# Attention and routed experts on one core: where the value product stands among the scores

## The chip, the cores and the metric

The kernel runs on one core of one Trainium2 chip. The metric is the device time of one execution in microseconds (us); of several runs the median is taken. Engines are TensorE (PE in the profile, its weight loads PEld), VectorE (DVE), ScalarE (ACT), GpSimd (POOL) and SyncE (SP).

## What is computed

A transformer layer on x of 8 x 512 x 128: attention with 16 heads of width 8, a residual and a layer norm, then 8 routed experts of which each token takes two, one shared expert, a residual and a layer norm. The change lies in the attention; the projection is reshaped in such a way that a head of the reference is a block of 32 rows of x with 16 columns of heads in it.

```python
qkv = (x @ w_qkv + b_qkv).reshape(B, N_HEADS, S, 3 * HEAD_DIM)
q, k, v = jnp.split(qkv, 3, axis=-1)
scores = jnp.einsum('bhqd,bhkd->bhqk', q, k) * scale
attn = jax.nn.softmax(scores, axis=-1)
vals = jnp.einsum('bhqk,bhkd->bhqd', attn, v)
vals = vals.transpose(0, 2, 1, 3).reshape(B, S, N_HEADS * HEAD_DIM)
x = layernorm(x + vals @ w_out + b_out)
x = layernorm(x + ffn(x))
```

## The kernel before

Four heads are a *quad*; there are 32, four to a batch of 512 tokens. All engines run the same list of stages (`run_stages`, L318), one per quad, with a few ahead of the first and one behind the last. Stage q does three things at once: the scores A of quad q+2 (`scoreA`, L1012), of which VectorE takes the maxima over the keys (L946); the scores B of quad q (`scoreB`, L1026), which are the same scores with keys and queries exchanged and the maximum subtracted by two more rows of the operands, and which ScalarE exponentiates into `prob` (L919); and the value product of quad q-1 (`pvp`, L1051), in fp32, four heads side by side in the columns of TensorE's array, summed over four chunks of keys in one PSUM bank.

A stage has 8 steps (`at` 0 to 7); head j = at // 2, half u = at % 2. TensorE's program (`attention_tensor`, L986) is an order written out by hand: in each step score A, score B, score A, score B, then the step's *jobs*, and in the odd steps (u = 1) behind them four matmuls of the value product. The two scores B of a step go to the two banks of `scoreB`, c = 0 and c = 1. A score B waits until the exponential of the score that used its bank before is done (L1025):

```python
need(pe, exp_done, 16 * q + 2 * at + c - 1)
```

A score A waits for the maxima of the step before the last (L1011). The value product of step 1 waits for the exponentials of the stage before, for the values (`v_ready`) and for the copy of the last product out of PSUM (`pv_copied`, L1047 to L1049).

The jobs share one PSUM bank, `shared`; a job starts only when the one before was read (`job_read`, L509). `Jobs.at` (L74) says which job stands in which step:

- step 0: the output projection `proj` (L542), in the third quad of a batch;
- step 1: `mT`, the transposition of the maxima (L530), read by VectorE, which writes them negated (L605, L607); SyncE then stores them into the operand rows (L760) and goes on to the loads of the stacks `qs` and `ks` for quad q+3 (L776, L780);
- step 2: `counts` of the router (L503, L504), in the second quad of a batch;
- step 3: `valsT`, the transposition of a finished value product (L534), which VectorE divides by the sums (L593, L599);
- step 4: `xT`, the transposition of a tile of x (L512);
- step 5: `x1T` (L547), in the fourth quad of a batch; ScalarE copies it (L578);
- step 6: `qkv`, the projections for a later quad (L518, L519, L523), which ScalarE reads with three instructions (L568, L572);
- step 7: `oT` (L537), in the second quad, read by a ScalarE copy (L576); `gate` (L553), in the fourth, read by a ScalarE exponential (L582).

ScalarE's program (`attention_scalar`, L899) starts each stage with the copy of the value product of the stage before out of `pvp` (L911), which waits for its last matmul (`pv_done`), and goes on with the 16 exponentials, with the jobs that it reads behind those of their step. VectorE's (`attention_vector`, L932) takes one pair of maxima per step and then that step's jobs and the router's or the norm's small operations. An engine runs its instructions in the order of its program. The experts follow when the attention is done, on the same core; the change does not touch them.

Of the kernel before, what the change touches and what calls it, by code (L numbers as in the profile page):

```python
# [110 lines left out]
def layer(nc, x, w_qkv, b_qkv, w_out, b_out, wg, ws1, ws3, ws2, we1, we3, we2, out):  # L111
# [26 lines left out]
    with ctx:  # L138
        def sb(name, shape, dt=F32):
            return ctx.enter_context(nc.sbuf_tensor(name, shape, dt))  # L140

        def psum(name, shape):
            return ctx.enter_context(nc.psum_tensor(name, shape, F32))

        def sem(name):
            return ctx.enter_context(nc.semaphore(name))
# [42 lines left out]
        v = sb("v", [P, 2, 4, NCH, 32])  # L189
        prob = sb("prob", [P, 2, 4, NCH, 512])  # L190
# [52 lines left out]
        pvp = psum("pvp", [P, 512])  # L243
# [23 lines left out]
        v_ready = sem("v_ready")  # L267
        b_ready = sem("b_ready")
        exp_done = sem("exp_done")
        pv_done = sem("pv_done")  # L270
        pv_copied = sem("pv_copied")
# [24 lines left out]
        def need(eng, s, value):  # L296

            if isinstance(value, int) and value <= 0:
                return
            eng.wait_ge(s, value)  # L300
            if not isinstance(value, int) and eng.engine in ALONE:


                eng.sem_inc(passed, 1)

        def has(b, i, ahead):

            return not isinstance(b, int) or 0 <= 4 * b + i + ahead < QUADS
# [9 lines left out]
        def run_stages(eng, stage):  # L318

            for s in range(-4, 8):  # L320
                stage(s // 4, s % 4)
            with eng.Fori(2, B - 1) as b:
                for i in range(4):
                    stage(b, i)
            for s in range(QUADS - 4, QUADS + 1):
                stage(s // 4, s % 4)
# [355 lines left out]
        def turn_x(pe, b):  # L682

            pe.wait_ge(x1_loaded[b], 16)

            need(pe, xT_low_done, b)
            for c in range(NCH):
                ins = pe.transpose(xT_bank[:, c * P:(c + 1) * P], xsum[:, b, c, :], ident[:])
            ins.then_inc(xT_ready, 1)
# [296 lines left out]
        def attention_tensor(pe):  # L986

            pe.wait_ge(setup, 2)
            for n in range(4):
                pe.matmul(pvp[:, 0:P], ident[:], ident[:], start=True, stop=True)  # L990

            def warm(times, columns):

                for n in range(times):
                    pe.matmul(pvp[:, 0:columns], wq[:], w_raw[:].rearrange("p c k d -> p (c k d)")[:, 0:columns],  # L995
                              start=True, stop=True)

            def stage(b, i):
                q = 4 * b + i
                if isinstance(b, int) and q == -2:  # L1000
                    warm(8, 3 * P)
                if has(b, i, 2):

                    pe.wait_ge(stack_loaded[i % 2], 16 * STACK_DMAS * (2 * b + i // 2 + 2))
                def score_a(at, c):

                    if has(b, i, 2):
                        st, j, qc = (i + 2) % 4, at // 2, at % 2 * 2 + c

                        if c == 0:  # L1010
                            need(pe, max_done, 8 * (q + 2) + at - 1)  # L1011
                        ins = pe.matmul(scoreA[:, at % 2, c], qs[0:KR, st, j, qc * P:(qc + 1) * P],  # L1012
                                        ks[0:KR, st, j, :], start=True, stop=True)
                        if c == 1:
                            ins.then_inc(a_ready, 1)

                def score_b(at, c):

                    if has(b, i, 0):
                        j, kc = at // 2, at % 2 * 2 + c  # L1020
                        if at == 0 and c == 0:

                            pe.wait_ge(m_loaded, 32 * (q + 1))

                        need(pe, exp_done, 16 * q + 2 * at + c - 1)  # L1025
                        pe.matmul(scoreB[:, c], ks[0:KM, i, j, kc * P:(kc + 1) * P], qs[0:KM, i, j, :],  # L1026
                                  start=True, stop=True).then_inc(b_ready, 1)

                for at in range(8):
                    j, u = at // 2, at % 2  # L1030
                    score_a(at, 0)
                    score_b(at, 0)
                    score_a(at, 1)
                    score_b(at, 1)
                    for kind, bb, ii in jobs.at(b, i, at):
                        if kind == "xT" and isinstance(b, int) and q == -3 and at == 7:
                            warm(1, 3 * P)
                        pe_job(pe, kind, bb, ii)
                    if isinstance(b, int) and q in (-2, -1) and not jobs.at(b, i, at) or \
                            isinstance(b, int) and q == 0 and u:  # L1040
                        warm(1, 2 * P)

                    if isinstance(b, int) and q == QUADS and at == 4:
                        turn_x(pe, 0)
                    if u == 1 and has(b, i, -1):
                        if j == 0:
                            pe.wait_ge(exp_done, 16 * q)  # L1047
                            pe.wait_ge(v_ready, q)
                            need(pe, pv_copied, q - 1)  # L1049
                        for h in range(4):  # L1050
                            ins = pe.matmul(pvp[32 * h:32 * h + 32, :], v[:, (i - 1) % 2, h, j, :],  # L1051
                                            prob[:, (i - 1) % 2, h, j, :], start=(j == 0), stop=(j == 3))
                        if j == 3:
                            ins.then_inc(pv_done, 1)

            run_stages(pe, stage)


# [601 lines left out]
```

## Time and profile before

| | |
|---|---|
| median of 3 runs | 690.12 us (687.95 to 690.82) |
| the profiled execution | 686.2 us, of which its span is 684.5 |
| busy: PE, DVE, ACT, POOL | 640.4, 548.9, 424.2, 269.4 us (94, 80, 62 and 39% of the span) |
| scores A, scores B, value products on PE | 512 x 386 ns, 512 x 387 ns, 1024 x 611 ns |
| exponentials on ACT | 512 x 600 ns, 278.7 us |
| maxima on DVE | 256 x 1219 ns, 304.5 us |
| mean granted clock of TensorE | 0.980 |

Matmuls are pipelined, and the profile models their ends; so the distance from one start to the next says more than a duration, and a busy TensorE may be one that waits. The starts are read from timelines, whose columns are: start in us, length of the group in us, engine, line, operation, what it writes and reads, shapes, and the number of instructions; in brackets stands how long the engine was idle before it and what ended that.

### The profile page before, as it was taken

Reading aid. Unit: us, or ns where it says so; the run is one execution under the profiler, and the core shown is the slowest. Engines: PE = TensorE matmul, PEld = TensorE weight load, DVE = VectorE, ACT = ScalarE, POOL = GpSimd, SP = SyncE. Lnnn points to the kernel's source line nnn. Section 1 sums busy time; section 2 is a strip of 40 time slices with the busy share of each in tenths; the row PEclk is TensorE's granted clock in tenths of the full one; section 3 lists DMA queues with packets and bytes.
Section 4 is the critical chain, followed back from the end, with each engine's and each line's share of the span. In section 5 each row is a group of like instructions: output and inputs, shape, how many; then the busy total and the mean of one; then the engine's idle time right before and its main releaser. Section 6 shows DMA issues by size and latency. Waiting matters only on the chain.

```text
span 684.5 us, 16202 instructions
## 1 busy us (share of the span) xinstructions
PE 640.4 (94%) x4653; PEld 320.8 (47%) x4653; DVE 548.9 (80%) x1272; ACT 424.2 (62%) x973; POOL 269.4 (39%) x402
## 2 busy tenths in 40 slices
PE   8899999999999999999999999999899989999970
PEld 5442333333334333333343334333258878888760
DVE  4895677779897997998899799797667767888882
ACT  2065677776676776677767667766734346666752
POOL 3322112333144335314434432540525526677772
PEclk9998899999999999999999999999999999999995
DMA  4557466344433324442333342330132033444522
GB/s 84 122 122 175 100 137 156 82 88 105 74 84 79 84 50 78 96 89 62 85 72 64 89 101 53 66 89 15 52 108 63 32 83 88 146 141 132 164 74 77
DMA packets 161857, 62.68 MB, mean 92 GB/s; under 512 B 110586, under 2 KB 155516, under 8 KB 161808
## 3 DMA queue, kind: packets, MB, share of 16 engines
q1 hardware_dynamic: 155008, 46.72, 31.2%
q0 software_dynamic: 5648, 13.26, 6.4%
q10 hardware_dynamic: 1152, 2.10, 0.8%
q8 instruction: 24, 0.39, 0.2%
q14 instruction: 25, 0.20, 0.1%
HBM read 38.04 MB, written 24.26 MB: 91 GB/s over the span
## 4 chain that ended last, share of the span: by engine, by line
PE 64%; issue 11%; POOL 8%; DVE 7%; DMA 4%; ACT 4%; SPq 2%; POOLq 0%; ACTq 0%; DVEq 0%
PE pvp L1051 16%; PE scoreB L1026 15%; PE scoreA L1012 14%; POOL y_dram L1242 6%; DVE mx L946 4%; DMA parts_dram<-parts 3%; ACT prob L919 2%; PE shared L534 2%; PE scoreB L1527 2%; PE shared L523 2%; PE pvp L995 1%; PE shared L518 1%; PE shared L553 1%; POOL prob L1227 1%; PE shared L542 1%
## 5 line engine op out<-in xcount | busy, mean ns | idle before, releaser
L919 ACT ACTIVATE prob<-scoreB 128x512 f32<-128x512 f32 x512 | 278.7, 600 | 125.9 <-PE scoreB L1026 125.5
L946 DVE TENSOR_REDUCE mx<-scoreA 128x2 f32<-128x1024 f32 x256 | 304.5, 1219 | 65.1 <-PE scoreA L1012 62.5
L1026 PE MATMUL scoreB<-qs,ks 74*128 74x512 bf16 x512 | 197.0, 387 | 6.4 <-ACT prob L919 3.0
L1012 PE MATMUL scoreA<-ks,qs 72*128 72x512 bf16 x512 | 195.2, 386 | 4.7 <-DMA ks<-parts_dram 2.4
L1051 PE MATMUL pvp<-prob,v 128*32 128x512 f32 x1024 | 137.6, 611 | 0.8 <-ACT pv_sb L911 0.8
L1012 PEld LDWEIGHTS scoreA<-ks,qs 72*128 72x128 bf16 x512 | 49.6, 99 | 138.9 <-DVE mx L946 65.1
L1026 PEld LDWEIGHTS scoreB<-qs,ks 74*128 74x128 bf16 x512 | 49.3, 97 | 100.3 <-ACT prob L919 77.6
L1242 POOL DMA_INDIRECT y_dram<-prob x72 | 70.8, 983 | 44.2 <-issue 30.7
L497 POOL DMA_INDIRECT slots_dram<-rows,slot_i x64 | 63.3, 990 | 56.5 <-DMA ks<-parts_dram 31.4
L846 POOL CAST parts<-qk 128x256 bf16<-128x256 f32 x32 | 12.7, 396 | 180.9 <-ACT v_raw L572 169.6
L1601 PE MATMUL scoreB<-w,prob 128*128 x288 | 44.2, 276 | 1.1 <-DVE prob L1414 1.1
L1470 ACT ACTIVATE prob<-scoreA 128x256 f32<-128x256 f32 x72 | 27.6, 383 | 22.4 <-PE pvp L1589 10.7
L1601 PEld LDWEIGHTS scoreB<-w,prob 128*128 128x128 f32 x288 | 37.8, 191 | 1.5 <-issue 1.3
L1579 PE MATMUL scoreA<-w_high,ebT_high 128*128 x72 | 34.5, 480 | 3.5 <-DVE gated L1418 3.5
L1418 DVE TENSOR_TENSOR gated<-scoreA,prob 128x256 f32<-128x256 f32 x72 | 30.2, 420 | 7.9 <-ACT prob L1470 7.4
L1051 PEld LDWEIGHTS pvp<-prob,v 128*32 128x32 f32 x1024 | 20.4, 108 | 29.4 <-issue 27.8
L1477 ACT ACTIVATE prob<-scoreB,prob 128x128 f32<-128x128 f32 x72 | 26.6, 369 | 11.7 <-PE scoreA L1559 9.3
L568 ACT ACTIVATE qk<-shared,bq 128x128 f32<-128x128 f32 x64 | 20.0, 363 | 18.7 <-PE shared L523 11.1
L645 POOL TENSOR_SCALAR veps<-mv 128x4 f32<-128x4 f32 x8 | 1.8, 227 | 73.2 <-DVE mv L627 73.2
L1348 DVE TENSOR_TENSOR ebT_low<-scoreA,ebT_high 128x128 fp32r<-128x128 f32 x72 | 20.8, 290 | 10.4 <-ACT ebT_high L1444 8.6
L1581 PE MATMUL scoreA<-w_high,ebT_low 128*128 x72 | 28.4, 395 | 0.0
L1580 PE MATMUL scoreA<-w_low,ebT_high 128*128 x72 | 28.3, 394 | 0.0
(178 smaller groups left out, 921.0 us busy)
## 6 DMA issues: line engine op xcount, KB each, us to landing
qs<-parts_dram SPq DMA_DIRECT2D x96, 96.0 KB
parts_dram<-parts SPq DMA_DIRECT2D x32, 192.0 KB
slots_dram<-blank POOLq DMA_DIRECT2D x9, 520.0 KB, 7.2
prob<-slots_dram SPq DMA_DIRECT2D x72, 65.0 KB, 1.9
ks<-parts_dram SPq DMA_DIRECT2D x64, 64.0 KB
prob<-y_dram SPq DMA_DIRECT2D x8, 512.0 KB, 3.3
ks<-parts_dram SPq DMA_DIRECT2D x32, 96.0 KB
xin<-in_L_attn_x SPq DMA_DIRECT2D x32, 64.0 KB, 2.2
```

The lines of the kernel that those rows point to most:

```text
L497: pool.indirect_dma_start(slots_dram, bass.IndirectOffsetOnAxis(ap=slot_i[:, j, t:t + 1], axis=0), rows[:, t, j, :], None).then_inc(scatte ...
L919: act.activation(prob[:, i % 2, j, 2 * u + c, :], scoreB[:, c], ACT.Exp, scale=SCALE).then_inc(exp_done, 1)
L946: dve.tensor_reduce(mx[:, i % 2, at // 2, at % 2 * 2:at % 2 * 2 + 2], scoreA[:, at % 2], AX.X, ALU.max).then_inc(max_done, 1)
L1012: ins = pe.matmul(scoreA[:, at % 2, c], qs[0:KR, st, j, qc * P:(qc + 1) * P], ks[0:KR, st, j, :], start=True, stop=True)
L1026: pe.matmul(scoreB[:, c], ks[0:KM, i, j, kc * P:(kc + 1) * P], qs[0:KM, i, j, :], start=True, stop=True).then_inc(b_ready, 1)
L1051: ins = pe.matmul(pvp[32 * h:32 * h + 32, :], v[:, (i - 1) % 2, h, j, :], prob[:, (i - 1) % 2, h, j, :], start=(j == 0), stop=(j == 3))
L1242: pool.indirect_dma_start(y2_dram, bass.IndirectOffsetOnAxis(ap=eb[:, at, D:D + 1].bitcast(I32), axis=0), yo[:, r, :], None, bounds_check= ...
L1418: dve.tensor_tensor(gated[:, r % 4, :], h_bank(r)[:, F:2 * F], silu[:, r % 2, :], ALU.mult) \
L1579: pe.matmul(h, ebT_highs[:, r % 4], high, start=True, stop=False)
L1580: pe.matmul(h, ebT_highs[:, r % 4], low, start=False, stop=False)
L1581: ins = pe.matmul(h, ebT_lows[:, r % 4], high, start=False, stop=True)
L1601: ins = pe.matmul(y_bank(r), gatedT[:, (r - 4) % 4, c * P:(c + 1) * P], w2_flat[:, bass.ds(e * NFC * D + c * D, D)], start=(c == 0), stop= ...
```

## The change

In the odd steps of a stage the four matmuls of the value product are issued between the second score A and the second score B (the last one of the step, c = 1). The step's job and, in the ramp, the warming matmuls, which stood in front of the value product, now stand behind that score B. Even steps stay as they are, and so do the programs of all other engines.

```diff
--- before.py
+++ after.py
@@ -1026,23 +1026,9 @@
                         pe.matmul(scoreB[:, c], ks[0:KM, i, j, kc * P:(kc + 1) * P], qs[0:KM, i, j, :],
                                   start=True, stop=True).then_inc(b_ready, 1)
 
-                for at in range(8):
-                    j, u = at // 2, at % 2
-                    score_a(at, 0)
-                    score_b(at, 0)
-                    score_a(at, 1)
-                    score_b(at, 1)
-                    for kind, bb, ii in jobs.at(b, i, at):
-                        if kind == "xT" and isinstance(b, int) and q == -3 and at == 7:
-                            warm(1, 3 * P)
-                        pe_job(pe, kind, bb, ii)
-                    if isinstance(b, int) and q in (-2, -1) and not jobs.at(b, i, at) or \
-                            isinstance(b, int) and q == 0 and u:
-                        warm(1, 2 * P)
-
-                    if isinstance(b, int) and q == QUADS and at == 4:
-                        turn_x(pe, 0)
-                    if u == 1 and has(b, i, -1):
+                def value_product(j):
+
+                    if has(b, i, -1):
                         if j == 0:
                             pe.wait_ge(exp_done, 16 * q)
                             pe.wait_ge(v_ready, q)
@@ -1052,6 +1038,25 @@
                                             prob[:, (i - 1) % 2, h, j, :], start=(j == 0), stop=(j == 3))
                         if j == 3:
                             ins.then_inc(pv_done, 1)
+
+                for at in range(8):
+                    j, u = at // 2, at % 2
+                    score_a(at, 0)
+                    score_b(at, 0)
+                    score_a(at, 1)
+                    if u == 1:
+                        value_product(j)
+                    score_b(at, 1)
+                    for kind, bb, ii in jobs.at(b, i, at):
+                        if kind == "xT" and isinstance(b, int) and q == -3 and at == 7:
+                            warm(1, 3 * P)
+                        pe_job(pe, kind, bb, ii)
+                    if isinstance(b, int) and q in (-2, -1) and not jobs.at(b, i, at) or \
+                            isinstance(b, int) and q == 0 and u:
+                        warm(1, 2 * P)
+
+                    if isinstance(b, int) and q == QUADS and at == 4:
+                        turn_x(pe, 0)
 
             run_stages(pe, stage)
 
```

## Rows read from the trace of the kernel before

**Rows 1.** The waits: engine, line, releaser: us in total, times, longest.

```profile
ACT prob L919 <- PE scoreB L1026: 125.5, 117, 10.2
...
PEld scoreB L1026 <- ACT prob L919: 77.6, 176, 1.2
```

**Rows 2.** Timeline of TensorE over the seam between a third and a fourth quad.

```profile
308.09 0.38 PE L1026 MATMUL scoreB<-qs,ks 74*128 74x512 bf16 x1
...
309.91 0.38 PE L1026 MATMUL scoreB<-qs,ks 74*128 74x512 bf16 x1
...
310.34 0.38 PE L1026 MATMUL scoreB<-qs,ks 74*128 74x512 bf16 x1
310.65 1.06 PE L1051 MATMUL pvp<-prob,v 128*32 128x512 f32 x8
...
311.88 0.38 PE L1026 MATMUL scoreB<-qs,ks 74*128 74x512 bf16 x1
...
313.00 0.39 PE L1026 MATMUL scoreB<-qs,ks 74*128 74x512 bf16 x1
...
313.50 0.39 PE L1026 MATMUL scoreB<-qs,ks 74*128 74x512 bf16 x1
...
313.93 1.06 PE L1051 MATMUL pvp<-prob,v 128*32 128x512 f32 x8
...
315.15 0.38 PE L1026 MATMUL scoreB<-qs,ks 74*128 74x512 bf16 x1
...
316.22 0.39 PE L1026 MATMUL scoreB<-qs,ks 74*128 74x512 bf16 x1
```

**Rows 3.** Timeline of ScalarE: the same seam, and one with a gate.

```profile
267.74 0.20 ACT L582 ACTIVATE ge<-shared 128x32 f32<-128x32 f32 x1 [0.27 <-PE shared L553]
...
310.57 1.09 ACT L919 ACTIVATE prob<-scoreB 128x512 f32<-128x512 f32 x2
311.87 0.60 ACT L911 ACTIVATE pv_sb<-pvp 128x512 f32<-128x512 f32 x1 [0.20 <-PE pvp L1051]
312.36 2.16 ACT L919 ACTIVATE prob<-scoreB 128x512 f32<-128x512 f32 x4
```

**Rows 4.** Timeline of TensorE: other seams, and jobs in the first and second quad.

```profile
263.89 0.38 PE L1026 MATMUL scoreB<-qs,ks 74*128 74x512 bf16 x1
...
266.55 1.06 PE L553 MATMUL shared<-w_g,valsT 128*128 128x8 f32 x8
...
269.90 0.39 PE L1026 MATMUL scoreB<-qs,ks 74*128 74x512 bf16 x1
...
276.28 0.28 PE L512 MATMUL shared<-ident,xin 128*128 128x128 f32 x1
...
286.76 0.40 PE L503 MATMUL shared<-both,lower 128*128 128x32 f32 x2 [0.17 <-DVE m L607]
...
293.04 0.38 PE L1026 MATMUL scoreB<-qs,ks 74*128 74x512 bf16 x1
...
295.69 0.66 PE L537 MATMUL shared<-ident,vals 128*128 128x128 f32 x4
...
298.16 1.05 PE L542 MATMUL shared<-w_o,valsT 128*128 128x128 f32 x8
...
299.27 0.38 PE L1026 MATMUL scoreB<-qs,ks 74*128 74x512 bf16 x1
```

**Rows 5.** Timeline of VectorE in the first quad of a batch.

```profile
271.69 0.27 DVE L605 TENSOR_SCALAR m<-shared 16x128 bf16<-16x128 f32 x1
...
275.81 0.29 DVE L599 TENSOR_TENSOR vals<-shared,rden 128x128 f32<-128x128 f32 x1
```

**Rows 6.** Stretches: length, PE, PEld, DVE, ACT, POOL busy, clock, DMA, GB/s.

```profile
62.20:80.20 18.00, 18.00 (x107) 5.93 (x108) 10.63 (x12) 9.86 (x20) 1.88 (x4) 0.72 0.69 164
...
282.30:297.30 15.00, 14.72 (x119) 5.58 (x116) 13.76 (x32) 10.54 (x23) 5.97 (x12) 1.00 0.42 84
```

**Rows 7.** Timeline of TensorE at the start of quad 2.

```profile
62.18 0.39 PE L1012 MATMUL scoreA<-ks,qs 72*128 72x512 bf16 x1 [1.58 <-DMA ks<-parts_dram]
```

More of the change, by code:

```diff
@@ L1027, in score_b @@
                                   start=True, stop=True).then_inc(b_ready, 1)
+                def value_product(j):
+                    if has(b, i, -1):
+                        if j == 0:
+                            pe.wait_ge(exp_done, 16 * q)
+                            pe.wait_ge(v_ready, q)
+                            need(pe, pv_copied, q - 1)
+                        for h in range(4):
+                            ins = pe.matmul(pvp[32 * h:32 * h + 32, :], v[:, (i - 1) % 2, h, j, :],
+                                            prob[:, (i - 1) % 2, h, j, :], start=(j == 0), stop=(j == 3))
+                        if j == 3:
+                            ins.then_inc(pv_done, 1)
                 for at in range(8):
@@ L1044, in stage @@
                         turn_x(pe, 0)
-                    if u == 1 and has(b, i, -1):
[L1046 to L1054, printed above, removed]
             run_stages(pe, stage)
```

## The prediction

> **What bounds the kernel now.** I read the waits first: they name the two engines that hold each other up. ScalarE waits 125.5 us for scores of the second kind (B, the ones that are exponentiated), TensorE 77.6 us for exponentials [rows 1]. So I read the two engines' timelines side by side over the end of one quad and the start of the next [rows 2, 3]; there every start is an event that can be followed. (0,0) is the first B of step 0, (7,1) the second of step 7, a prime marks the next quad.
>
> The reader is to see four things in rows 2 and 3.
> - Undisturbed, a score follows the one in front after 0.22 (two of them lie between (7,0) at 309.91 and (7,1) at 310.34). A value product begins 0.31 after a bare score (310.34 to 310.65) and 0.43 after one with the maxima's transposition between (313.50 to 313.93), so that job is worth 0.12. From its start to the next quad's first B, with a score A between, pass 1.23: 1.00 of its own and 0.22.
> - A PSUM bank of B is free again 1.07 after its last B began: 315.15 to 316.22, four spacings of 0.22 and 0.19 of idling. Two banks alternate, so each bank has one B per step.
> - ScalarE does an exponential every 0.54 (2.16 for four), begins the first 0.42 after its B, and does the copy of the value product in program order between the last exponential of a quad and the first of the next: copy at 311.87, first exponential 0.49 later at 312.36, and TensorE's B of step 1 another 0.64 later at 313.00.
> - Against its place in the order, that B is late: four spacings behind 311.88 it could start at 312.76, so TensorE idles 0.24 there.
>
> Within a quad TensorE is therefore bound by its own work and by one bank reuse per pair of steps, and at the seam between quads by the copy.
>
> **The change, part by part.** No instruction is added or removed; per quad four value products change places with the last B of their odd steps, and the odd steps' jobs go behind that B. No DMA is issued by TensorE; SyncE's queue is touched only through the maxima's job.
>
> *A pair inside a quad.* Before, from the odd step's first B to the next even step's first: 313.00 to 315.15, 2.15 [rows 2]. After: 0.22 to A, 0.31 to the product, 1.00, then the B (0.22, its bank long free), the job 0.12, A 0.22: 2.09. The job cancels, so 0.06 is gained in each of three pairs: the B that stood 0.50 instead of 0.44 behind its neighbour no longer waits. 28 quads with both kinds of score (2 to 29): 28 x 3 x 0.06 = -5.0 us.
>
> *What becomes late in bank 1.* Before, the product stood between (5,1) and (6,1). After, they are 0.88 apart where step 5 has no job, and the bank needs 1.07: +0.19 in step 6, and everything behind it shifts. Behind the transposition (0.12) the lack is 0.07, and it is hidden by the wait for bank 0 that follows.
>
> *The seam.* Zero is (6,0) at 308.09. Before: (7,0) 1.82, (7,1) 2.25, product 2.56, copy 3.78, (1',0) 4.91 [rows 2, 3]. After: (7,0) 2.01, A 2.23, product 2.54, (7,1) 3.54, its exponential 3.96, copy 4.50, first exponential of the new quad 4.99, (1',0) 5.63. So +0.72. The copy no longer runs in ScalarE's idle time behind the product: it queues behind an exponential whose score is itself queued behind the product. It holds for the 15 seams without a TensorE job in step 7 while both kinds of score run (behind quads 2, 4, ..., 28, and behind 3): 15 x 0.72 = +10.8.
>
> *Seams with a job.* Behind quads 5, 9, ..., 29 the transposition oT stands in step 7 and the projection in step 0'. Before, (6,0) to (1',0) is 6.23 [rows 4]. After: (7,1) 3.54, oT 3.76, read by ScalarE after the exponential at 4.50, projection released at 5.15, and 1.11 from there to (1',0) as now (298.16 to 299.27): 6.26, +0.03. oT also loses the wait it has today, for the values' read: it starts 2.65 after (6,0), and (7,1) stands at 2.25. 7 seams, with some more at the last: +0.4. Behind quads 7, ..., 27 the gate stands there (before 6.01, [rows 4]), and in step 5 the x1 transposition with a ScalarE copy. After, that copy holds the job of step 6 by some 0.06, so (7,0) is at 1.87, (7,1) 3.40, gate 3.62, its end 1.06 later, its read of 0.20 [rows 3] from about 4.8, copy 5.0, (1',0) 6.13: 6 x 0.12 = +0.7.
>
> *Other waits that the moved jobs make.* The maxima's transposition comes 1.0 later on TensorE; VectorE, which in the first quad of a batch begins their negation 1.79 after (1,0) (271.69 against 269.90, [rows 4, 5]), gets it only at 2.08, +0.29. Behind it on VectorE are the router's operations, two maxima and the division of the values. That ends at 276.10 and the input's transposition in step 4 follows at 276.28 [rows 4, 5]: 0.18 of room, less 0.15 by which TensorE now comes sooner (what the two pairs in front gain in this quad), so with 0.04 for the signal (an exponential ends 0.60 after its start, the B it frees starts at 0.64) a wait of 0.30. Four spacings and that transposition, taken at 0.12 like the other, fill 1.00 of the bank's 1.07, so 0.07 of it is hidden: 5 x 0.23 = +1.2 in the quads 8, 12, ..., 24. Bounds: 0, and 0.6 for each if VectorE is late by as much again; I take the walk. In the second quad of a batch the counts now wait 0.17 for the maxima's read [rows 4]; since (2,1) comes relatively later, I take back 0.15 of it, between 0 and 0.3: 6 x -0.15 = -0.9. The maxima's rows go to SyncE, whose queue holds the stack loads behind them: only quad 2 waits for such a load, 1.58 [rows 7], and it would come 0.3 later: +0.3. Elsewhere it is hidden by most of a quad. In quads 30 and 31 there are no A scores; job and seam there pull in opposite directions, I take 0, bounds -1 and +1.4 (two seams).
>
> **Sum.** -5.0 + 10.8 + 0.4 + 0.7 + 1.2 - 0.9 + 0.3 = +7.5 us. On the profiled execution (686.2, of which 684.5 span) that is 693.7; this one is 3.9 below the median of the runs, 690.12, and I add the sum to the median: **697.6 us**, 1.1% slower.
>
> One price deserves a second look: the 0.09 by which a product starts later than a score would (0.31 against 0.22). I keep it behind A, the trace showing it only behind B [rows 2]. The Trainium skill, "TensorE: Matmul & The Clock Gate", section "Step-by-step: what each phase is for", says that TensorE pulls weight loads ahead of running matmuls, when their row groups do not conflict or the background buffer takes them. By that the product would start 0.22 after any score, and the sum would fall by 10 us if the rule held behind A alone. The rows behind B show that it does not hold there.
>
> **The rivals.**
> - *Not slower: the weights of the product load under score A.* Place: A to product, four times in each of 28 quads; price 28 x 4 x 0.09 = -10.1, less some of it at the seams that wait for ScalarE anyway; sum -2.6, 687.5 us. It decides from about 0.07 a product. For it: A has 72 rows, B 74, so the loads need not be alike. Against: the 0.09 behind B in rows 2 stands where no other engine holds the product. 0.09.
> - *No change: the seam is half as dear.* If the exponential of (7,1) or the copy starts sooner than I chain them, or (6,1) is not held, the seam costs 0.35: 15 x -0.37 = -5.6, so 692.0 us. For it: ends of matmuls are modelled. Against: 0.42, 0.54, 0.49 and 0.64 all are distances of starts. 0.16.
> - *VectorE becomes the bound.* It is busy 13.76 of 15.00 us in a second quad of a batch [rows 6]; the jobs now reach it later. If its 0.29 showed in two quads of each of six batches: 12 x 0.29 = +3.5, 701.1 us. Against: every start in rows 2 and 4 is explained by TensorE's own order, an exponential or a job's read, none by a score A that lacks its bank, and the longer seam gives VectorE time. 0.12.
> - *TensorE's clock falls.* After the 1.58 us wait for a load the granted clock of quad 2 was 0.72 in the mean, part of it at the lower level (1.2 GHz), and the quad took 18.00, against 15.00 for the longest kind of the others [rows 6, 7]: 3.0 us or more. The new idling at a seam, 0.19 and 0.6, is shorter and in two pieces. If one or two quads more fell: 700.6 to 703.6 us. 0.07.
>
> **How the numbers follow.** The walk as it stands, 695 to 700.5 us, has 0.56. About 0.5% (3.5 us) is what a measurement of this kernel can tell from no change: 686.7 to 693.6. Faster: a third of the first rival and a few hundredths for what I do not see: 0.07. Same: the rest of the first, most of the second, and the low tail of the walk: 0.22. Slower: 0.71. The range takes in the half-price seam and the VectorE case and leaves out the first rival's lower half and the second fall of the clock: 688 to 703.5.
>
> **What would show it.** Right: in the timeline of the changed kernel the copy of the value product starts about 0.54 after the last exponential's start and not 0.2 behind the product; TensorE idles 0.6 in front of (1',0); (6,1) starts 0.62 behind (6,0); pairs inside a quad take 0.06 less; ScalarE's one long wait per pair of steps splits into two. Wrong: a product 0.22 behind its A, a copy that overlaps the product's tail, VectorE as releaser of scores A, or a lower clock in more than one quad.

## The result and the profile after

The changed kernel takes 698.86 us in the median (695.28 to 703.9, 4 runs), the kernel before 689.04 (684.34 to 690.82, 4 runs) beside it: a ratio of 1.0162, 95% interval 1.0113 to 1.0211. It is slower, by 9.8 us. The profiled execution took 699.3 us, its span is 697.6; that is 13.1 more than the profiled execution before.

The first view is the page of the changed kernel, its busy times, and then its waits (engine, line, releaser: us in total, times, longest), which answer to [rows 1]:

```profile
PE 644.5 (92%) x4653; PEld 317.4 (46%) x4653; DVE 554.5 (79%) x1272; ACT 433.0 (62%) x973; POOL 269.6 (39%) x402
```

```profile
PEld scoreB L1026 <- ACT prob L919: 175.3, 269, 1.2
ACT prob L919 <- PE scoreB L1026: 137.6, 179, 10.2
...
PE scoreB L1026 <- ACT prob L919: 11.1, 25, 0.7
...
PEld scoreA L1012 <- DVE mx L946: 8.1, 16, 1.0
```

Two lines of the kernel before, for comparison:

```profile
PEld scoreA L1012 <- DVE mx L946: 65.1, 84, 1.0
...
PE scoreB L1026 <- ACT prob L919: 3.0, 6, 0.7
```

The number of instructions is the same, and so is the work. What grew is the time in which TensorE's next B waits for an exponential: its weight loads (PEld) wait 175.3 us at 269 places where it was 77.6 at 176. Much of that runs beside matmuls, whose ends are modelled; with no matmul running it is 11.1 us instead of 3.0. ScalarE's waits for scores became more and shorter, 179 for 137.6 us instead of 117 for 125.5. VectorE holds hardly any score A: 8.1 us instead of 65.1.

The timeline of TensorE at the same kind of seam as in [rows 2], behind quad 18 (start, length, engine, line, operation, operands, count; in brackets idle time and releaser):

```profile
315.51 0.38 PE L1026 MATMUL scoreB<-qs,ks 74*128 74x512 bf16 x1
315.72 0.38 PE L1012 MATMUL scoreA<-ks,qs 72*128 72x512 bf16 x1
316.14 0.39 PE L1026 MATMUL scoreB<-qs,ks 74*128 74x512 bf16 x1
...
317.52 0.38 PE L1026 MATMUL scoreB<-qs,ks 74*128 74x512 bf16 x1
317.74 0.38 PE L1012 MATMUL scoreA<-ks,qs 72*128 72x512 bf16 x1
318.05 1.07 PE L1037 MATMUL pvp<-prob,v 128*32 128x512 f32 x8
319.05 0.39 PE L1026 MATMUL scoreB<-qs,ks 74*128 74x512 bf16 x1
...
320.36 0.38 PE L1012 MATMUL scoreA<-ks,qs 72*128 72x512 bf16 x1
321.11 0.39 PE L1026 MATMUL scoreB<-qs,ks 74*128 74x512 bf16 x1 [0.37 <-ACT prob L919]
...
323.20 0.38 PE L1026 MATMUL scoreB<-qs,ks 74*128 74x512 bf16 x1
```

And the timeline of ScalarE there, which answers to [rows 3]:

```profile
318.19 0.61 ACT L919 ACTIVATE prob<-scoreB 128x512 f32<-128x512 f32 x1
319.48 0.60 ACT L919 ACTIVATE prob<-scoreB 128x512 f32<-128x512 f32 x1 [0.68 <-PE scoreB L1026]
319.97 0.59 ACT L911 ACTIVATE pv_sb<-pvp 128x512 f32<-128x512 f32 x1
320.45 1.68 ACT L919 ACTIVATE prob<-scoreB 128x512 f32<-128x512 f32 x3
```

The weight loads of the last A of step 7 and of the product at this seam:

```profile
317.52 0.10 PEld L1012 LDWEIGHTS scoreA<-ks,qs 72*128 72x128 bf16 x1
...
318.05 0.16 PEld L1037 LDWEIGHTS pvp<-prob,v 128*32 128x32 f32 x8 [0.43 <-issue]
```

This is the walk of the prediction. With (6,0) at 315.51 as zero, (6,1) comes 0.63 behind it (forecast 0.62), (7,0) at 2.01 (2.01), the product at 2.54 (2.54), (7,1) at 3.54 (3.54), its exponential at 3.97 (3.96), the copy at 4.46 (4.50), the next quad's first exponential at 4.94 (4.99) and (1',0) at 5.60 (5.63), against 4.91 before. TensorE could have started (1',0) 0.22 behind 320.36; it waits from 320.58 to 321.11, 0.53, and the copy stands in front of the exponential that it waits for. From there to (2,0) it takes 2.09, 0.06 less than before.

What the profile has and the walk has not is the clock. TensorE behind a seam with the gate, quads 15 to 16, and the stretches around it (length, then PE, PEld, DVE, ACT and POOL busy, granted clock, DMA share, GB/s):

```profile
274.47 0.38 PE L1012 MATMUL scoreA<-ks,qs 72*128 72x512 bf16 x1
275.55 0.39 PE L1026 MATMUL scoreB<-qs,ks 74*128 74x512 bf16 x1 [0.70 <-ACT prob L919]
275.78 0.50 PE L1012 MATMUL scoreA<-ks,qs 72*128 72x512 bf16 x1
276.21 1.94 PE L1037 MATMUL pvp<-prob,v 128*32 128x512 f32 x8
278.08 0.61 PE L1026 MATMUL scoreB<-qs,ks 74*128 74x512 bf16 x1
```

```profile
274.00:276.00 2.00, 1.30 (x6) 0.31 (x4) 1.23 (x1) 1.66 (x5) 1.54 (x4) 0.98 0.00 0
276.00:279.00 3.00, 3.00 (x12) 0.62 (x12) 1.23 (x1) 0.85 (x2) 2.35 (x3) 0.50 0.63 72
```

TensorE was busy for 1.30 of 2.00 us, and then the granted clock is at its lower level (0.50, 1.2 GHz): the product takes 1.87 instead of 1.00. The same is seen behind quad 19. The idling in front, from 0.22 behind the A at 274.47 to 275.55, was 0.86 us in one piece. The Trainium skill, "TensorE: Matmul & The Clock Gate", section "A second HAM failure mode: psum-queue depth-cycling", says that many small idle stretches between groups of matmuls can make the clock go down and up. The trace agrees only in part: no long idling stood in front, but the one piece is not many small ones. Now ScalarE at the same seam, and below it why TensorE's wait is longer there:

```profile
272.99 0.60 ACT L919 ACTIVATE prob<-scoreB 128x512 f32<-128x512 f32 x1 [0.38 <-PE scoreB L1026]
273.88 0.20 ACT L582 ACTIVATE ge<-shared 128x32 f32<-128x32 f32 x1 [0.29 <-PE shared L553]
274.41 0.60 ACT L911 ACTIVATE pv_sb<-pvp 128x512 f32<-128x512 f32 x1 [0.34 <-issue]
```

Between the gate's exponential and the copy ScalarE is idle for 0.34 us for which the profile names no releaser. In the kernel before the copy at this seam waited for the product's end:

```profile
268.76 0.60 ACT L911 ACTIVATE pv_sb<-pvp 128x512 f32<-128x512 f32 x1 [0.83 <-PE pvp L1051]
```

From the starts of the scores B in the two timelines, quad by quad over quads 4 to 28, the difference comes apart like this (us, sums over the quads). A pair runs from the first B of an odd step to the first B of the next step; the rest of a seam runs from (7,0) to (1',0), so that step 6 stands by itself:

| term | forecast per place | measured per place | sum |
|---|---|---|---|
| three pairs in each quad | -0.06 | -0.05 to -0.10 | -4.4 |
| step 6, bank 1 late | +0.19 | +0.21, and 0.13 in fourth quads | +4.6 |
| rest of 13 seams without a job | +0.53 | +0.50 | +6.4 |
| rest of 6 seams with oT | with step 6 +0.03 | with step 6 -0.03 | -1.4 |
| rest of 6 seams with the gate | with step 6 +0.12 | with step 6 +0.32 | +1.2 |
| input's transposition | +0.23 in 5 first quads | 0.32 in those with a full clock, 0.1 in third quads | +1.5 |
| counts | -0.15 | -0.06 | -0.3 |
| falls of the clock, quads 16 and 20 | 0 | about 1.4 | +2.9 |

Without the falls these are +7.6, with them +10.5. The -1.4 of the seams with oT is in part an accident of the profile before, in which TensorE waited behind quad 9 for a stack load:

```profile
180.75 0.39 PE L1012 MATMUL scoreA<-ks,qs 72*128 72x512 bf16 x1 [0.79 <-DMA ks<-parts_dram]
```

The other five of these seams, with step 6, are 0.09 to 0.17 longer than before. Quads 1 to 3, with the waits for the first loads and the fall of the clock behind them, add 2.3 in this pair of profiles; that stretch took between 42.6 and 49.3 us (from the maxima's transposition of quad 1 to that of quad 4) in the profiles of this study, whatever the kernel, and nothing is read from it.

### The profile page after: what moved, and what is told of

Read it like the earlier page. It is cut to its first block, busy times and chain, and to the rows that moved or that the text cites. A ratio compares the mean times of both kernels' runs of the same rounds, so it can differ in the third digit from the quotient of the medians.

```text
span 697.6 us, 16202 instructions
## 1 busy us (share of the span) xinstructions
PE 644.5 (92%) x4653; PEld 317.4 (46%) x4653; DVE 554.5 (79%) x1272; ACT 433.0 (62%) x973; POOL 269.6 (39%) x402
## 4 chain that ended last, share of the span: by engine, by line
PE 59%; issue 11%; POOL 10%; DVE 8%; ACT 5%; DMA 4%; SPq 1%; ACTq 0%; POOLq 0%; DVEq 0%
PE pvp L1037 17%; PE scoreB L1026 17%; PE scoreA L1012 12%; POOL y_dram L1247 6%; DVE mx L946 3%; ACT prob L919 2%; DMA parts_dram<-parts 2%; PE shared L534 2%; PE shared L523 2%; DMA ks<-parts_dram 1%; PE shared L542 1%; ACT pv_sb L911 1%; POOL prob L1232 1%; PE shared L518 1%; POOL slots_dram L497 1%
## 5 line engine op out<-in xcount | busy, mean ns | idle before, releaser
L919 ACT ACTIVATE prob<-scoreB 128x512 f32<-128x512 f32 x512 | 290.8, 600 | 138.3 <-PE scoreB L1026 137.6
L1026 PE MATMUL scoreB<-qs,ks 74*128 74x512 bf16 x512 | 199.0, 390 | 14.1 <-ACT prob L919 11.1
L1037 PE MATMUL pvp<-prob,v 128*32 128x512 f32 x1024 | 139.3, 618 | 0.9 <-ACT pv_sb L911 0.9
L1026 PEld LDWEIGHTS scoreB<-qs,ks 74*128 74x128 bf16 x512 | 49.7, 97 | 197.5 <-ACT prob L919 175.3
```

Of the source, the lines that this page charges most:

```text
L919: act.activation(prob[:, i % 2, j, 2 * u + c, :], scoreB[:, c], ACT.Exp, scale=SCALE).then_inc(exp_done, 1)
```

## The experiments

**Three of four products moved.** The product of step 7 goes back to its old place.

```diff
-                    if u == 1:
+                    if at in (1, 3, 5):
                         value_product(j)
                     score_b(at, 1)
...
+                    if u == 1 and at not in (1, 3, 5):
+                        value_product(j)
```

> The product stands in front of the last B in steps 1, 3 and 5 and back at its old place in step 7. Theory (the seam is dear because the copy of the product queues behind an exponential whose B comes late): the 0.49 per bare seam goes, as does the dear seam behind the gate; left are the pairs (-0.05 x 3 x 28 = -4.2), the 0.20 in step 6 (28 x 0.20 = +5.6, less where a job stands in step 5) and the input transposition's wait (+1.5): about +2 us on the kernel before, 690 to 692 us. Rival (every moved product costs by itself): three of four are still moved, so three quarters of the +9.8, about +7, 696 us.

Measured: 691.32 us (10 runs), before 688.03 (29 runs), ratio 1.0052 (1.0013 to 1.0092): by the ratio +3.6, where the seam's theory said +2 and the rival +7. The interval, +0.9 to +6.3, holds the first and leaves the second just out; the trace says more. Behind quad 18 the copy waits for the product again, as before the change:

```profile
315.26 0.60 ACT L911 ACTIVATE pv_sb<-pvp 128x512 f32<-128x512 f32 x1 [0.20 <-PE pvp L1037]
```

Over quads 4 to 28 its profile is 2.5 us behind the one before. The rests of the seams add up to 0.03, against 6.2 in the changed kernel; the pairs give -4.6 and step 6 costs +4.6, about as there, and the input's transposition costs +2.2. So the pairs, step 6 and the seam are three terms, and they can be taken apart.

**Only the product of step 7 moved.** The same edit with `at in (7,)`.

> Only the product of step 7 is moved. Theory of the seam: no bank 1 is late in step 6, but (7,1) of the seam stands behind the product and the copy behind its exponential: 15 bare seams x 0.5 = +7.5, the gate's seams x 6 about +0.4 = +2.4, oT's 7 x -0.1: about +9 us on the kernel before, 698 us. No gain in the pairs. Rival (every moved product costs by itself): a quarter of +9.8, 691.5 us.

Measured: 699.73 us (4 runs, 692.18 to 702.79; 697.91 without the longest) against 688.03, ratio 1.0198 (1.0122 to 1.0274). Within the spread of the runs one moved product of four costs as much as all four. ScalarE at the seam behind quad 18:

```profile
312.63 0.60 ACT L919 ACTIVATE prob<-scoreB 128x512 f32<-128x512 f32 x1 [0.68 <-PE scoreB L1026]
313.12 0.59 ACT L911 ACTIVATE pv_sb<-pvp 128x512 f32<-128x512 f32 x1
```

The copy queues behind the exponential, as in the changed kernel. The profiled execution is the shortest of the four. Over quads 4 to 28 it is 9.0 us behind the one before: the rests of the seams are +6.2, as in the changed kernel, step 6 is unchanged (0.0), and two falls of the clock, in quads 16 and 20, add 3.0. The rival, a quarter of the loss, falls.

**The copy behind the first exponential.** The changed kernel; ScalarE does the first exponential of the new quad ahead of the copy of the product.

```diff
-                    act.activation(pv_sb[:], pvp[:], ACT.Copy).then_inc(pv_copied, 1)
...
                                 act.activation(prob[:, i % 2, j, 2 * u + c, :], scoreB[:, c], ACT.Exp,
                                                scale=SCALE).then_inc(exp_done, 1)
+                                if j == 0 and u == 0 and c == 0:
+                                    copy_product()
...
```

> The changed kernel, with ScalarE's copy of the product behind the first exponential of the new quad instead of in front of it; nothing else moves. Theory of the seam: the 0.49 between the last exponential of a quad and the first of the next goes wherever TensorE waited for it: 15 bare seams x -0.49 and some -0.4 in each of 6 seams with the gate, -9 to -10 on the changed kernel, and with it the falls of the clock behind two gates (-2.6 in the profile): 687 to 690 us, about the kernel before. Rival (the late B at (7,1) is the cost and the copy is hidden): no change against the changed kernel, 697 to 699 us.

Measured: 687.08 us (12 runs) against 688.03, ratio 1.0002 (0.9967 to 1.0038). The loss is gone within what these runs can tell. ScalarE at a seam without a job, in its timeline:

```profile
309.99 1.08 ACT L922 ACTIVATE prob<-scoreB 128x512 f32<-128x512 f32 x2 [0.67 <-PE scoreB L1031]
310.96 0.60 ACT L912 ACTIVATE pv_sb<-pvp 128x512 f32<-128x512 f32 x1
311.44 1.11 ACT L922 ACTIVATE prob<-scoreB 128x512 f32<-128x512 f32 x2
```

The last exponential of the old quad and the first of the new follow each other (two in 1.08 us), and the copy comes behind them, where TensorE waits for nothing of it. The rests of the 13 seams without a job cost 0.6 us in all, of 6.4. The late score at (7,1) is the same here; it is not the cost by itself. This kernel keeps all four moved products and step 6's +4.6; at the six seams with the gate the rests fall from +1.2 to -1.4, and no fall of the clock shows from quad 4 on. Over quads 4 to 28 its profile is 1.5 behind the one before.

**Steps 1 and 3 only, the maxima's transposition in front.**

```diff
+                    if at == 1:
+                        for kind, bb, ii in jobs.at(b, i, at):
+                            pe_job(pe, kind, bb, ii)
+                    if at in (1, 3):
                         value_product(j)
                     score_b(at, 1)
...
```

> The product stands in front of the last B in steps 1 and 3 only, in step 1 with the maxima's transposition still in front of it; steps 5 and 7 as before. Theory: the two pairs keep their gain (2 x 28 x -0.055 = -3.1), no bank 1 is late in step 6, the seam is as before, and VectorE gets the maxima at the old time so that the input's transposition does not wait: 686 to 687 us, 0.4% faster than the kernel before. Rival (the gain of 0.05 per pair is given back by the bank of the next even step): the kernel before, 689 us.

Measured: 686.97 us (12 runs) against 688.03, ratio 1.0001 (0.997 to 1.0033). The theory is not borne out: no gain that can be measured. The second pair keeps its -1.5 over quads 4 to 28. In the first the gain is lost: in third quads the transposition waits for VectorE's read of the projection, and now it waits in front of the product instead of behind a score (+0.2 each); elsewhere (3,0) comes 0.05 later, since (1,1) and with it its exponential stands closer to (2,0). The input's transposition still waits, by 0.1 in third and fourth quads, for the division of the values, whose own transposition is still behind, and 0.06 of that comes back in the next pair; in first quads about 0.02 is left of 0.32, so there the wait came from the maxima's.

**ScalarE without a loop.** The changed kernel; ScalarE's stages are written out.

```diff
-            run_stages(act, stage)
+            for s in range(-4, QUADS + 1):
+                stage(s // 4, s % 4)
             x_high(act, 0)
```

> The changed kernel with ScalarE's stages written out instead of looped over the batches; the instructions of a stage are the same. Theory: the 0.34 us in which ScalarE waits for nothing between the gate's exponential and the copy of the product, in four seams of the changed kernel and in none of the other two with a gate, is its step from one pass of the loop to the next. It goes, and the four seams come to the 4.2 us from (7,0) to (1',0) of the two others, 0.3 less each: -1.2 us on the changed kernel, and less falls of the clock behind the gate. Rival (ScalarE waits there for something of the gate or the copy): the 0.34 stays with the straight program.

Measured: 692.88 us (6 runs) against 688.02 (13 runs), ratio 1.0097 (1.0056 to 1.0138); the changed kernel beside it 699.38. ScalarE at a seam with the gate:

```profile
267.28 0.60 ACT L919 ACTIVATE prob<-scoreB 128x512 f32<-128x512 f32 x1 [0.50 <-PE scoreB L1027]
268.07 0.20 ACT L582 ACTIVATE ge<-shared 128x32 f32<-128x32 f32 x1 [0.20 <-PE shared L553]
268.16 0.59 ACT L911 ACTIVATE pv_sb<-pvp 128x512 f32<-128x512 f32 x1
```

The idle time of 0.34 is gone: it was the step from one pass of the loop to the next. (7,0) to (1',0) is 3.98 at all six seams with the gate, against 4.51 to 4.54 at the four where the changed kernel's loop turns and 4.15 and 4.21 at the two where ScalarE enters the loop or leaves it. That is 0.2 more than the 0.34 at each turn, which I had not expected. The starts say where 0.1 of it lies: the copy now begins 0.09 behind the start of the gate's exponential, while that still runs, instead of 0.53 (273.88 to 274.41). The other 0.1 is the gate's exponential itself, which comes that much sooner; why, no run here shows. It sums to -2.6 on the changed kernel over quads 4 to 28, and there is no fall of the clock there in its profile.

**The idle time behind the gate filled.** The changed kernel, with three matmuls whose result nothing reads, in front of the first B of step 1 in the first quads of batches 2 to 7.

```diff
                     score_a(at, 0)
+                    if at == 1 and i == 0 and (not isinstance(b, int) or 2 <= b < B):
+                        need(pe, job_read, jobs.number("mT", b, i))
+                        for n in range(3):
+                            pe.matmul(shared[:], qs[0:KR, (i + 2) % 4, 0, 0:P], ks[0:KR, (i + 2) % 4, 0, :],
+                                      start=True, stop=True)
```

> The changed kernel with three matmuls more that nothing reads, 0.22 us each, in front of the first B of step 1 in the first quads of batches 2 to 7, where TensorE idles 0.7 to 0.9 us behind a gate. Theory: the two quads of the profile in which the granted clock fell to half behind that idling, 1.2 to 1.4 us longer each, are its consequence; filled, the clock stays and the changed kernel gains 1 to 3 us in the median at no cost of the matmuls. Rival (the falls have another cause): the clock falls as often, the same time as the changed kernel or longer.

> The changed kernel again, beside the others of this call: 697 to 699 us, 1.4% above the kernel before, with one to three falls of the clock in a run.

Measured: 697.22 us filled (6 runs), 699.38 for the changed kernel again (6 runs), before 688.02 (13 runs); ratios 1.0126 (1.0087 to 1.0165) and 1.0172 (1.013 to 1.0215). TensorE at the seam between quads 15 and 16, filled:

```profile
274.99 0.38 PE L1012 MATMUL scoreA<-ks,qs 72*128 72x512 bf16 x1
275.21 0.81 PE L1048 MATMUL shared<-ks,qs 72*128 72x512 bf16 x3
276.07 0.39 PE L1026 MATMUL scoreB<-qs,ks 74*128 74x512 bf16 x1
276.30 0.38 PE L1012 MATMUL scoreA<-ks,qs 72*128 72x512 bf16 x1
276.61 1.06 PE L1037 MATMUL pvp<-prob,v 128*32 128x512 f32 x8
277.61 0.39 PE L1026 MATMUL scoreB<-qs,ks 74*128 74x512 bf16 x1
```

(1',0) comes 1.08 behind the A in front, as without the three, and the product takes its 1.00: the clock stays. In this profile it is full from quad 4 to 28, while the changed kernel's second profile has falls behind three gates. Over quads 4 to 28 the filled kernel is 8.6 behind the kernel before, the changed one 10.5 in the first profile and 16.0 in the second. The medians differ by 2.2 us as expected, but their intervals overlap, and a single profile stands for the filled kernel. In the three profiles of kernels with the moved product of step 7 in the loop and nothing in this idle time (the changed kernel's two and that of step 7 alone) the clock fell at 7 of the 12 seams where the loop turns, in the filled one at none of 4. So the traces point to the idle time as the cause, and the times agree; they do not settle it.

**One job into the idle time.** The kernel before, with the transposition of the finished product in step 2 instead of 3, but for second quads, which have the counts in step 2.

```diff
-        if at == 3 and (inner or 0 <= s - 2 < self.quads):
+        if at == (3 if i == 1 else 2) and (inner or 0 <= s - 2 < self.quads):
             kinds.append("valsT")
```

> The kernel before, with the transposition of the finished product (0.44 us on TensorE) one step earlier, in step 2 in place of step 3, but for the second quad of a batch, which has the counts there. Theory (a bank of B is free 1.07 us after its last B began, four spacings fill 0.88, so 0.19 of each even-to-odd step is idle where no job stands in it): 0.19 of the job falls into that idle time, in 3 of 4 quads: 24 x -0.19 = -4.5 us, 683.5 us where the kernel before has 688. Rival (the idle time is hidden by what follows, or VectorE, which reads the job, has it too early behind its maxima): no change, 688 us.

Measured: 681.34 us (6 runs) against 688.02, ratio 0.9911 (0.9876 to 0.9947): the one kernel here that is faster than both. TensorE's steps 2 and 3 in a third quad:

```profile
299.61 0.38 PE L1026 MATMUL scoreB<-qs,ks 74*128 74x512 bf16 x1
...
300.27 0.60 PE L534 MATMUL shared<-ident,pv_sb 128*128 128x128 f32 x4
...
300.93 0.38 PE L1026 MATMUL scoreB<-qs,ks 74*128 74x512 bf16 x1
...
301.67 1.06 PE L1051 MATMUL pvp<-prob,v 128*32 128x512 f32 x8
...
302.90 0.38 PE L1026 MATMUL scoreB<-qs,ks 74*128 74x512 bf16 x1
```

The same starts of B in the kernel before:

```profile
301.45 0.38 PE L1026 MATMUL scoreB<-qs,ks 74*128 74x512 bf16 x1
...
302.52 0.39 PE L1026 MATMUL scoreB<-qs,ks 74*128 74x512 bf16 x1
...
304.99 0.38 PE L1026 MATMUL scoreB<-qs,ks 74*128 74x512 bf16 x1
```

From (2,0) to (4,0) it is 3.29 instead of 3.54. (3,0) is 1.32 behind (2,0), more than the bank's 1.07, so TensorE no longer idles there, and (3,1) is free of its wait too: 0.25 saved per quad, where I had counted 0.19. In 24 quads that makes 6.0, of the 6.7 between the medians. The profiled execution is the longest of the six; over quads 4 to 28 it is 3.5 ahead of the one before, with a wait of 1.45 for a stack load behind quad 8 in it.

## Why the prediction was right, and where it was off

- *A pair gains 0.06.* Right, -0.05 to -0.06 in most and up to -0.10 in first pairs.
- *Bank 1 is late in step 6, +0.19.* Right: 0.21, and with three products moved it stays when the seam is undone.
- *The seam, +0.72 with step 6.* Right: 0.70, place by place within 0.05. That the copy in ScalarE's program order makes it is shown from both sides: step 7 alone brings the rest of the seam back in full, and the copy placed one exponential later takes nearly all of it away with every product still moved.
- *The first rival, weights of the product loaded under A.* Wrong: the product starts 0.31 behind its A (317.74 to 318.05), as it did behind B [rows 2]. The weight loads shown above say the same: A's stands 0.22 ahead of its matmul, the product's first at the product's own start. The rule of the Trainium skill that the prediction weighed ("TensorE: Matmul & The Clock Gate", section "Step-by-step: what each phase is for") shows for the scores and does not show for the product.
- *The second rival, a seam of half the price,* and *the third, VectorE as the bound,* did not come: waits of scores A for maxima fell from 65.1 to 8.1 us.
- *Seams with the gate, +0.12.* Mis-sized: +0.32 in the mean. Where the loop turns, (1',0) comes 6.45 to 6.48 behind (6,0), at the other two seams 6.09 and 6.15, where the walk said 6.13. The step that failed is the copy at 5.0: at the turns it comes 0.3 later (5.31 at the seam shown). The walk took ScalarE's gaps from seams where the copy waits for the product's end, 0.83 at this one, which hid the turn of its loop. Without the loop (7,0) to (1',0) is 3.98 at all six.
- *Only quad 2 waits for a stack load.* Misread: the profile before has the wait of 0.79 behind quad 9 as well, and in the profiles of this study such waits come and go, most of them in the first quads.
- *The fourth rival, the clock,* had 0.07 and came beside the main case: two quads in one profile, three in the other, always at a seam with the gate where the loop turns, with an idle time of 0.85 to 0.88. I had held the new waits for too short; the 0.6 that I weighed is that of the other seams. A fall cost 1.3 to 4.4 us in the two profiles; I had given it 3.0.
- *The sum, +7.5.* Its places within quads 4 to 28 were forecast at +6.2 and measure +7.6 with a full clock; the gate's seams make +1.2 of the difference, and the others nearly cancel. With the falls, which the sum put at nothing, the profile has +10.5 there. The medians differ by 9.8, and how much of that is falls was not taken apart. That 698.86 lies so close to the 697.6 of the forecast is in part luck: the median of the kernel before came out 1.1 lower than the one that the sum was added to.

## What to carry to other kernels

When two engines hand buffers to each other, list for each buffer the shortest time from one use to the next (here 1.07 us) and what stands between in the program of each engine. Taking work out from between two uses only pays if enough is left there to fill that time; put small jobs where it is not filled, as the run with the transposition in step 2 does. And look at the seam of a loop on the other engine: an instruction that used idle time there, like the copy, gets onto the path as soon as what is in front of it in its queue comes later.

## What had not been expected of the hardware

- At the turn of its loop ScalarE is idle for 0.33 to 0.36 us without a releaser in the profile, and 0.53 us of the seam's time went with it when the stages were written out (4.51 to 3.98).
- The granted clock fell to 0.50 behind some 0.86 us of idling where the gate's small matmuls (128x8) stood in front, not at every such seam and not in the same number of quads from profile to profile. Behind the waits of 0.50 to 0.55 at the other seams, two with the gate among them, it did not fall in any profile here. Not every fall had 0.86 in front: in the profile of the first experiment it fell in quad 29, behind a wait of 0.59 of the counts for a read by VectorE. In three profiles (the first experiment, the filled kernel, the job in step 2) it also fell behind the gate of quad 31, where no scores A are left; TensorE had waited 0.47 to 0.59 in front of that gate.
